# A four-layer transformer kernel on one core: VectorE takes all sums of the first attention's exponentials, and work at the seams of the later stages is put elsewhere

## What is computed

```
x = x + attention0(norm(x), ctx)     # 8 heads of 64, softmax over 1601 keys, Wo, bo
x = x + routed_experts(norm(x))      # 8 experts, sinkhorn gates
x = x + attention1(norm(x), ctx)     # one head of 256, mask
x = x + ternary_ffn1(norm(x))        # r = relu(bitlinear(x) + gate * low rank); bitlinear(r * r)
x = x + attention2(norm(x), ctx)     # one head of 256, biases
x = x + ternary_ffn2(norm(x))        # gelu between two ternary products with an RMS norm
x = x + attention3(norm(x), ctx)     # 16 heads of 16, mask, Wo, bo
x = x + expert_ffn3(norm(x))         # 8 blocks of 256 rows, gelu
```

## Time and profile before

| | us |
|---|---|
| median of 3 runs | 2548.96 |
| lowest and highest | 2537.8, 2552.43 |
| the profiled execution, its own time | 2549.59 |
| its span, first to last instruction | 2547.8 |

### The profile page before, as it was taken

The page is one execution under the profiler, slowest core; times in us unless marked ns, Lnnn a source line. Parts: engine busy times, 40 slices in busy tenths (PEclk is TensorE's granted clock), DMA queues, the critical chain, the costliest instruction groups (busy, mean ns, idle before and its releaser), DMA issues. The chain is left out here.

```text
span 2547.8 us, 35597 instructions
## 1 busy us (share of the span) xinstructions
PE 2292.0 (90%) x13628; PEld 1208.3 (47%) x13660; DVE 1621.6 (64%) x3450; ACT 1283.0 (50%) x1730; POOL 403.8 (16%) x302
## 2 busy tenths in 40 slices
PE   8999999999667858999889999786999999999888
PEld 3333323223322345777665777662444344443377
DVE  5566666674479744342653453775799989997385
ACT  3555555555258621223432222540577777877753
POOL 1244343444135520000000000001000000000011
PEclk9999999999778778999889999885899999998798
DMA  3000000000131141210010111003120101010142
GB/s 131 5 5 9 10 10 5 10 10 9 46 135 52 61 158 66 90 35 1 13 45 16 65 65 52 7 8 103 44 39 11 36 10 32 7 35 2 67 131 69
DMA packets 63504, 108.47 MB, mean 43 GB/s; under 512 B 13495, under 2 KB 45124, under 8 KB 62308
## 3 DMA queue, kind: packets, MB, share of 16 engines
q1 hardware_dynamic: 60884, 100.84, 12.8%
q0 software_dynamic: 1888, 4.42, 0.6%
q10 hardware_dynamic: 560, 0.92, 0.1%
HBM read 87.88 MB, written 17.73 MB: 41 GB/s over the span
## 5 line engine op out<-in xcount | busy, mean ns | idle before, releaser
L2740 DVE TENSOR_REDUCE pm<-PS 128x1 f32<-128x512 f32 x768 | 473.5, 684 | 46.5 <-PE PS L2585 45.4
L2703 ACT ACTIVATE P<-PS 128x1024 f32<-128x1024 f32 (+1 forms) x416 | 422.4, 1024 | 119.6 <-PE PS L2623 116.9
L2585 PE MATMUL PS<-Ks,Qs 49*128 49x512 f32 x768 | 301.5, 479 | 25.2 <-DMA Qs<-q_parts 17.6
L2623 PE MATMUL PS<-Qs,Ks 51*128 51x512 f32 (+1 forms) x832 | 309.7, 459 | 0.4 <-ACT P L2703 0.4
L734 ACT ACTIVATE P<-PS 128x1024 f32<-128x1024 f32 (+1 forms) x208 | 213.3, 1026 | 172.8 <-PE PS L642 161.8
L2643 PE MATMUL PS<-P,V 128*17 128x256 f32 (+2 forms) x3072 | 262.4, 414 | 8.2 <-ACT P L2703 7.3
L655 PE MATMUL PS<-P,V 128*64 128x512 f32 (+1 forms) x832 | 227.1, 624 | 4.7 <-ACT P L734 4.7
L2623 PEld LDWEIGHTS PS<-Qs,Ks 51*128 51x128 f32 (+1 forms) x832 | 127.2, 185 | 171.2 <-issue 139.0
L557 POOL TENSOR_TENSOR odd<-odd,P 128x1024 f32<-128x1024 f32 x64 | 159.6, 2493 | 177.6 <-ACT P L734 177.6
L2585 PEld LDWEIGHTS PS<-Ks,Qs 49*128 49x128 f32 x768 | 126.6, 193 | 61.6 <-DVE pm L2740 28.5
L635 PE MATMUL PS<-Qh,Kh 64*128 64x512 bf16 (+1 forms) x416 | 125.0, 390 | 0.0
(11 more groups left out here) (368 smaller groups left out, 4693.4 us busy)
## 6 DMA issues: line engine op xcount, KB each, us to landing
mi<-in_mask SPq DMA_DIRECT2D x32, 800.5 KB, 4.4
We<-in_L_ffn_w SPq DMA_DIRECT2D x16, 1024.0 KB, 7.5
Wg<-gate_rows SPq DMA_DIRECT2D x8, 1024.0 KB, 12.5
Qs<-q_parts SPq DMA_DIRECT2D x90, 64.0 KB, 2.9
Ks<-k_parts SPq DMA_DIRECT2D x24, 200.1 KB, 6.0
R<-denominators SPq DMA_DIRECT2D x30, 128.0 KB, 2.8
q_parts<-T SPq DMA_DIRECT2D x7, 512.0 KB, 2.7
k_parts<-Tk SPq DMA_DIRECT2D x6, 400.0 KB, 2.7
```

The costliest lines, as they stand in the source:

```text
L2585: m = e.matmul(PS[:, b, :], self.Qs[rows, s, pr, q0:q0 + 128], self.Ks[rows, s, pr, cs], start=True, stop=not masked)
L2623: m = e.matmul(ps, self.Ks[rows, s, pr, ks], self.Qs[rows, s, pr, q], start=True, stop=not masked)
L2703: e.activation(self.P[0:r, n % 4, :, :], PS[0:r, b:b + 2, :], ACT.Exp, scale=0.25).then_inc(*k.ac_exp.up((3, n)))
L2740: e.tensor_reduce(self.pm[:, u % 2, i, c:c + 1], PS[:, ring.of(("max", key)), :], AX.X, ALU.max).then_inc(*k.dv_max.up((3, *key)))
```

## The change

Six edits, in the order of the program.

1. A0: GpSimd has no part in the sum. VectorE adds every key tile from kt = 1 on into `acc`, PE's den reads `acc`, ScalarE's exponential waits for `acc` alone, and `odd` is gone. The bounds of divide and project move from 0.2, 0.64 and 0.66, 0.92 to 0.27, 0.7 and 0.71, 0.95.
2. At the end of C1, F1 and C2, PE and ScalarE no longer wait for the last update of X (`dv_x`); the first product that writes to the four output banks waits for it instead.
3. F1: low becomes three steps: split, low (z1) and low turn (z2), called head steps. F1 and F2: the head steps of block qb + 2 stand late in block qb, those of block 1 in the rise of block 0.
4. F1 and F2: the fall begins at 0.12 of the merged list for blocks 0 to 2, and the rise ends at 0.92.
5. Query parts (0, 0) to (0, 2) of A3 are projected, split and stored in F2, in F2's ring of banks and one buffer `T_early`; (0, 2) is the last step of F2. SP issues their stores. F2's barrier waits for these stores too.
6. A3: half of the row loads goes to SP, ahead of the keys, half to ScalarE, ahead of the queries of part (0, 0); GpSimd issues none. They have a semaphore for each half.

```diff
 class Program: leave
-    def leave(self, at, name):
+    def leave(self, at, name, x_later=False):
         if at.final and name in BARRIERS:
             for s, value in self.ends[name].items():
+                if x_later and name in X_LATER and s is self.dv_x:
+                    continue
...
 class L0Attention: order, tensor, scalar, vector
-                parts += [(self.divide_steps(u - 1), 0.2, 0.64), (self.project_steps(u - 1), 0.66, 0.92)]
+                parts += [(self.divide_steps(u - 1), 0.27, 0.7), (self.project_steps(u - 1), 0.71, 0.95)]
...
-            at.wait_ge(k.pl_done, ("sum", u))
+            at.wait_ge(k.dv_acc, ("A", u, KT - 1))
...
-                if kv % 2:
-                    at.wait_ge(k.pl_done, ("odd", v, max(3, kv)))
-                else:
-                    at.wait_ge(k.dv_acc, ("A", v, max(2, kv)))
+                at.wait_ge(k.dv_acc, ("A", v, max(1, kv)))
...
-        elif step == "attend" and key[1] % 2 == 0 and key[1]:
+        elif step == "attend" and key[1]:
...
-                at.wait_ge(k.dv_acc, ("A", u, kt - 2))
+                at.wait_ge(k.dv_acc, ("A", u, kt - 1))
...
 def ffn_order
-    out = ffn.rise_steps(0)
+    out = ffn.head_steps(0) + weave((ffn.rise_steps(0), 0.0, 1.0), (ffn.head_steps(1), 0.6, 0.95))
     for qb in range(4):
-        parts = [(ffn.fall_steps(qb), 0.0, 1.0), (aside[qb], 0.0, 0.9)]
+        parts = [(ffn.fall_steps(qb), 0.12 if qb < 3 else 0.0, 1.0), (aside[qb], 0.0, 0.9)]
         if qb < 3:
-            parts.append((ffn.rise_steps(qb + 1), 0.0, 1.0))
+            parts.append((ffn.rise_steps(qb + 1), 0.0, 0.92))
+        if qb < 2:
+            parts.append((ffn.head_steps(qb + 2), 0.62, 0.95))
...
 class L1Ffn (class L2Ffn: head_steps is the split alone)
+    def head_steps(self, qb):
+        return [(self, "split", (qb,)), (self, "low", (qb,)), None, (self, "low turn", (qb,))]
...
 class L3Attention
+        self.T_early = nc.alloc_sbuf_tensor_at("T3_early", [128, 2, 512], F32R, offset=P_at - 1472)
+        self.early, self.ring2 = [(0, 0), (0, 1), (0, 2)], ring2
...
+    def rows_load(self, e, at, o):
+        at.wait_ge(k.dv_misc, "row")
...
+        e.dma_start(Ks[o:o + 1, :, :], wide(row, M)).then_inc(*ld.up("mask", 16))
+        e.dma_start(Ks[o + 1:o + 3, :, :], wide(ones, M)).then_inc(*ld.up("ones", 16))
+        e.dma_start(Qs[o:o + 1, :, 0:M], wide(ones[0:1, :], M)).then_inc(*ld.up("q", 16))
+        e.dma_start(Qs[o:o + 1, :, M:N], wide(ones[0:1, :], N - M)).then_inc(*ld.up("all", 16))
...
 def stages
-    ffn2.aside = [[]] + spread(row3.steps(), 3)
-    out.append(("F2", row3.load_steps() + ffn2.order()))
+    aside = spread(row3.steps(), 3)
+    ffn2.aside = [[], aside[0]] + [[(att3, "part", (0, c))] + aside[c + 1] for c in range(2)]
+    out.append(("F2", row3.load_steps() + ffn2.order() + [(att3, "part", (0, 2))]))
```

More of the change, by code:

```diff
@@ L489, in order @@
                     if before[1] == KT - 1:
-                        out += [(self, "take", before[:1]), (self, "sum", before[:1])]
+                        out.append((self, "take", before[:1]))
                 before = (u, kt)
@@ L493, in order @@
                 later = later[1:]
-        out += [(self, "attend", before), (self, "take", before[:1]), (self, "sum", before[:1])]
+        out += [(self, "attend", before), (self, "take", before[:1])]
         return [s for s in out if s]
@@ L2020, in rise_steps, with head_steps @@
     def rise_steps(self, qb):
-        return [(self, "split", (qb,))] + [(self, "up", (qb, f)) for f in range(8)]
+        return [(self, "up", (qb, f)) for f in range(8)]
+    def head_steps(self, qb):
+        return [(self, "split", (qb,))]
     def fall_steps(self, qb):
@@ L2417, in order @@
         out = [(self, "begin", ()), (self, "rows load", ())] + self.key_loads(0)
[L2418 to L2421 removed]
+        out += self.query_loads(0, 0) + [(self, "value load", ()), (self, "load", ())]
+        rest = self.norms.steps(6, 3) + self.query_loads(0, 1) + self.query_loads(0, 2)
+        rest += [(self, "part", (0, 3))] + self.query_loads(0, 3)
         maxima = [s for u in range(16) for s in self.max_steps(u)]
@@ L2510, in sync @@
             e.dma_start(self.V[0:65, 12, :], self.keys.vd[1536:M, :]).then_inc(*self.ld_v.up("all", 16))
-        elif step == "part" and key != (0, 0):
+        elif step == "rows load":
+            self.rows_load(e, at, 112)
+        elif step == "part":
             self.store(e, at, key)
@@ L2568, in tensor @@
             half, c = key
-            b = ring.take(at, ("part", key))
+            b = (self.ring2 if key in self.early else ring).take(at, ("part", key))
             at.wait_ge(self.row.ld, "all")
@@ L2678, in scalar @@
             at.wait_ge(self.row.ld, "all")
-            if n > 1:
+            if key in self.early:
+                ring = self.ring2
+                if n:
+                    at.wait_ge(*self.stored(self.parts[n - 1]))
+            elif n > 4:
                 at.wait_ge(*self.stored(self.parts[n - 2]))
-            e.activation(self.T[:, n % 2, 0, :], PS[:, ring.of(("part", key)), :], ACT.Identity,
+            e.activation(self.tile(key)[:, 0, :], PS[:, ring.of(("part", key)), :], ACT.Identity,
                          bias=self.row.bq[:, half:half + 1]).then_inc(*k.ac_proj.up((3, "q", *key)))
-            if key == (0, 0):
-                self.store(e, at, key)
+        elif step == "rows load":
+            self.rows_load(e, at, 48)
         elif step == "query stack" and key[:2] == (0, 0):
@@ L2707, in scalar @@
             at.wait_ge(k.pe_out, (3, 13 * u + 12))
[L2708 removed]
+            for o in (48, 112):
+                at.wait_ge(self.ld_row[o], "all")
             if u > 1:
@@ L2729, in vector @@
             half, c = key
-            n = self.parts.index(key)
+            ring = self.ring2 if key in self.early else ring
+            T = self.tile(key)
             at.wait_ge(k.ac_proj, (3, "q", *key))
-            e.scalar_tensor_tensor(out=self.T[:, n % 2, 1, :], in0=PS[:, ring.of(("part", key)), :],
-                                   scalar=self.row.bq[:, half:half + 1], in1=self.T[:, n % 2, 0, :], op0=ALU.add,
+            e.scalar_tensor_tensor(out=T[:, 1, :], in0=PS[:, ring.of(("part", key)), :],
+                                   scalar=self.row.bq[:, half:half + 1], in1=T[:, 0, :], op0=ALU.add,
                                    op1=ALU.subtract).then_inc(*k.dv_proj.up((3, "q", *key)))
```

86 lines of the change are left out of this document (37 added, 49 removed).

## The result

| | before | after |
|---|---|---|
| median of four runs, us | 2545.99 | 2519.11 |
| lowest and highest, us | 2537.8, 2552.43 | 2509.91, 2522.72 |
| the profiled execution: time, span, us | 2549.59, 2547.8 | 2509.91, 2507.6 |
| mean granted clock of it | 0.917 | 0.926 |

The ratio is 0.9882, 95% interval [0.9854, 0.9911]: 30 us less, 23 to 37. The forecast was 2517, and the time is 2519. The total came out, but the parts it was summed from did not, and this document is mostly about that. The profiled execution of before lies high among its runs and that of after is the fastest of its four, so the two profiles differ by 40 us where the medians differ by 27.

What follows compares the result with a forecast made beforehand. PE was busy for 566.5 of 585 us in A0; elsewhere waits and the lower clock cost time. Terms -3.0 (A0), -12.0 (F1), -5.3 (F2), -11.8 (A3) sum to -32.1, from 2549.6 to 2517 us, range 2498 to 2543.

Steps and rivals of the forecast that it cites:

- 0.7 us of new waits a unit, 10 in all: A0: PE waits anew at the maxima because VectorE lags, +10 us, bounds 0 and 25.
- the slow rival: A0: VectorE becomes the bound; if 12 us of idling stay, +62 us in place of -3.0, 2583 us; chance 0.07.
- The waits at den, -10.7: A0: PE's waits for GpSimd's last sum, in 9 places, go: -10.7 us.
- The -2.3 for exponentials: A0: half of PE's 4.7 us of waits for exponentials goes, with P freed one tile earlier at a unit's head.
- A0 stays smooth: Rival for A0: VectorE's lag never reaches the ring, the 10 us of new waits fall away, 2507 us; chance 0.1.
- the waits for the out of the block before: F1: the later start of the fall removes two thirds of PE's 6.9 us in six places, -4.6 us.
- the other 4.6 go, and two thirds of 9.0: F2: PE's waits for xl away from the stage's head go, -4.6 us, and two thirds of those for X, -6.0.
- The charge for the two parts, 5.3: F2: added query parts (0, 0) and (0, 1) cost 3.8 us of PE and 1.5 of VectorE, charged in full.
- the same 15.3 for all: Head of A3: all loads land 15.3 us after the barrier, first maximum at 1735.8, -2.5 us; bounds 12 and 22 us.
- the first rival: Head of A3: row loads crowd a few DMA engines, taking 13.4 us instead of 8, total 2522 us; chance 0.2.
- The maxima: A3 after its first maximum: two of three query parts gone, -7.3 us of PE products and -2.0 of waits for T.
- the three signs: Prediction wrong if A0 is over 10 us longer, A3's head starts no earlier, or F1 and F2 together gain under 8.

Runs made afterwards that it cites:

- e4_sum_old_bounds: Kernel before with VectorE summing all key tiles of A0, but divide and projection bounds left as they were; ratio 0.9952, A0 564.3 us.
- rows_pool: Changed kernel with the row loads at the head of A3 issued by GpSimd again; ratio 0.9859.
- rows_dram: Changed kernel with rows stored to DRAM by GpSimd at the end of F2 and loaded by it as flat pieces cut in 16; ratio 0.9866.

## Why the prediction was right in its sum and wrong in its parts

By the ledger, means over the profiles of each kind (A0 as the two lengths that it had):

| term | forecast | measured |
|---|---|---|
| A0 | -3.0 | -17 to -22 |
| F1 | -12.0 | -6.2 to -16 (177.1 to 166.5 in the mean, -10.6) |
| F2 | -5.3 | +2.6 |
| seam | -2.5 | +3.8 (24.0 to 27.8 in the mean) |
| maxima | -9.3 | -8.1 |
| sum | -32.1 | -29 to -34; timed -30, interval -23 to -37 |

- **A0, the step that failed: "0.7 us of new waits a unit, 10 in all".** They did not come: PE waits 0.9 us in all for a bank of a maximum, and before it was 3.3. I had argued that VectorE's 5.4 us waits for Rc leave a lag in front of the maxima. But a VectorE with more to do reaches the reciprocal later and finds Rc there: 34.6 us of waiting in place of 81.3. I had written this very sentence as an argument against the slow rival and not used it in my own term. With the old bounds it is still 53.0 (e4_sum_old_bounds), so most of that is the added work and not the later reciprocal. The other part of the miss is the last three units, 8.4 us, where GpSimd's adds no longer hold up VectorE's short step for the norms, and through it ScalarE's exponential and PE, and where the clock fell once in place of three times. I saw line 801 held up and priced it as VectorE's work alone, 0.5 us a unit, with no one behind it; and I wrote that 18.5 us stood to be gained in A0 at most, taking its clock of 0.99 as no room, while 0.67 and 0.83 stood in its last stretches. 21.7 us came in the first pair of profiles. The waits at den, -10.7, were read rightly (a wait of 1.04 cost 1.26). The -2.3 for exponentials came too, 4.7 to 2.2, but not for the reason given, P freed earlier: that is luck. The rival "A0 stays smooth" had the mechanism, and gave A0 -13.
- **F1 was right in size.** -10.6 in the mean for -12.0, but more by clock and less by waits than I had it: 0.66 or 0.83 became 1.00 behind C1, and the waits for the out of the block before only fell from 6.9 to 4.3, with 2.6 new ones for z2's remainder.
- **F2 failed at "the other 4.6 go, and two thirds of 9.0".** The first did not go, 10.6 to 11.3; the second did, and as much came up at h and hT. The charge for the two parts, 5.3, was in size (2.6 to 4.6).
- **The seam failed at "the same 15.3 for all".** The barrier opened 6.1 us after the last down, as forecast; the loads then took 20.9 us, not 15.3. That is the first rival's case: it had 0.2, on a row that already showed 3.4 engines at work for 8 us; the order of the queues, which I held against it, only moved that stretch to the front. Its amount, 5.4 for a measured 5.6, is luck again: it came from a stretch of 13.4 us on two engines, and what stands there is 8 us with 2.9 at work, and keys and queries issued behind it.
- **The maxima** were right: 62.0 to 53.9 in the mean.

Of the signs I had named, these showed: line 798 near 1.22 us and line 781 near 0.2, no wait of PE at den for a sum, and the last product of F1's first up 6.1 us behind C1's last (1191.15 less 1185.05; forecast 5.5, before 9.4). These did not: 5 to 15 us of new waits in A0, a shorter F2, and 21 us from F2's last down to the first maximum. I had also said when the prediction would be wrong, and two of the three signs come close or come true: F1 and F2 together gained 8.0 us in the mean, just the 8 that I had set, and 2.9 in the first pair of profiles; and the head of A3 starts 3.8 us later behind F2's last down, though earlier in the kernel. By these signs the account of the seam, and on the first pair that of F1 and F2, was wrong.

So the forecast was too hopeful by 17 us in F2, seam, maxima and F1 together, and too fearful by 14 to 19 in A0. That 2517 met 2519 is luck, and the ledger is what should be believed. Of the versions tried, rows_pool (2515.49 against a before of 2552.94) and rows_dram (2511.91 against 2548.07) have the lowest ratios, but neither is told apart from the changed kernel.
